# A graph network's attention layers: accumulators kept per head, and a mask's penalty in PSUM

## The reference, cut to what matters

```python
def _gat_layer(x, src, dst, W, a_src, a_dst, b):
    h = (x @ W).reshape(N, H, C)                  # H = 4, C = 24
    alpha_s = jnp.einsum('nhc,hc->nh', h, a_src)
    alpha_d = jnp.einsum('nhc,hc->nh', h, a_dst)
    e = jax.nn.leaky_relu(alpha_s[src] + alpha_d[dst], NEG_SLOPE)
    m = jax.ops.segment_max(e, dst, num_segments=N)
    ex = jnp.exp(e - m[dst])
    den = jax.ops.segment_sum(ex, dst, num_segments=N)
    msg = h[src] * (ex / (den[dst] + 1e-16))[:, :, None]
    return jax.ops.segment_sum(msg, dst, num_segments=N).reshape(N, H * C) + b

x = _layernorm(x + message_layer(x))
y = x
for l in range(3):
    y = jax.nn.relu(_gat_layer(y, src, dst, W[l], att_src[l], att_dst[l], bias[l]))
x = _layernorm(x + y)
```

## Time and profile before

| | us |
|---|---|
| median of 3 runs | 8607.32 (8591.76 to 8612.24) |
| profiled execution | 8603.82 |
| its span | 8601.9 |

### The profile page before, as it was taken

The page is one execution under the profiler, slowest core; times in us unless marked ns, Lnnn a source line. Parts: engine busy times, 40 slices in busy tenths (PEclk is TensorE's granted clock), DMA queues, the critical chain, the costliest instruction groups (busy, mean ns, idle before and its releaser), DMA issues. The chain is left out here.

```text
span 8601.9 us, 131191 instructions
## 1 busy us (share of the span) xinstructions
PE 5700.5 (66%) x27740; PEld 5045.6 (59%) x27740; DVE 4467.6 (52%) x11640; ACT 3999.8 (46%) x8993; POOL 6236.4 (72%) x6545
## 2 busy tenths in 40 slices
PE   6999997777566666666656666666665666666663
PEld 2488886666555555555545555555554555555553
DVE  8977765555544444444444444444454444444446
ACT  5755554444344444444434444444443444444443
POOL 3677777777577777777667777777757777777775
PEclk7555555555566666666666666666666666666666
DMA  5222222222122222222222222222222222222221
GB/s 161 65 49 49 49 48 46 47 46 46 36 42 42 42 42 42 42 42 42 37 44 42 42 42 42 42 42 42 42 38 42 42 42 42 42 42 42 42 42 32
DMA packets 290250, 394.16 MB, mean 46 GB/s; under 512 B 176392, under 2 KB 183960, under 8 KB 287984
## 3 DMA queue, kind: packets, MB, share of 16 engines
q0 software_dynamic: 206976, 330.75, 20.1%
q1 hardware_dynamic: 61176, 46.25, 2.2%
q10 hardware_dynamic: 22024, 16.47, 0.8%
HBM read 367.38 MB, written 25.63 MB: 46 GB/s over the span
## 5 line engine op out<-in xcount | busy, mean ns | idle before, releaser
L637 POOL DMA_INDIRECT store<-table_a,idx x4851 | 4615.1, 951 | 1556.5 <-issue 1463.3
L1286 PE MATMUL ps<-store,work 128*128 x9744 | 1769.7, 352 | 945.1 <-ACT work L1218 942.5
L1286 PEld LDWEIGHTS ps<-store,work 128*128 128x128 f32 x9744 | 1646.2, 262 | 1132.3 <-issue 1128.1
L1269 PE MATMUL ps<-ident,work 128*128 128x128 f32 x4872 | 1148.9, 409 | 1371.7 <-ACT work L1225 1371.1
L779 POOL DMA_INDIRECT store<-table_m,idx x1617 | 1532.8, 948 | 615.1 <-issue 478.8
L1225 ACT ACTIVATE work<-work,small 128x896 f32<-128x896 f32 x696 | 725.1, 1042 | 2415.4 <-DVE store L1143 2379.3
L1269 PEld LDWEIGHTS ps<-ident,work 128*128 128x128 f32 x4872 | 920.4, 215 | 1453.8 <-issue 1359.3
L1151 DVE CUSTOM_DVE_ANT_0 work<-work,ps 128x896 f32<-128x896 f32 x696 | 756.6, 1087 | 1231.3 <-issue 937.8
L1162 DVE SCALAR_TENSOR_TENSOR work<-dstf,store,select 128x224 f32 x696 | 314.0, 451 | 1891.4 <-SPq L600 1887.5
L1277 PE MATMUL ps<-ident,work 128*128 128x128 f32 x4872 | 1090.3, 395 | 111.8 <-DVE work L1172 111.8
L1277 PEld LDWEIGHTS ps<-ident,work 128*128 128x128 f32 x4872 | 980.6, 217 | 115.4 <-DVE work L1172 115.4
(11 more groups left out here) (251 smaller groups left out, 5029.8 us busy)
## 6 DMA issues: line engine op xcount, KB each, us to landing
store<-table_a,idx POOLq DMA_INDIRECT x4851
store<-table_m,idx POOLq DMA_INDIRECT x1617, 2.5
work<-edge_parts ACTq DMA_DIRECT2D x232, 45.5 KB
edge_parts<-store SPq DMA_DIRECT2D x6, 1617.0 KB, 11.5
work<-edge_parts SPq DMA_DIRECT2D x50, 192.0 KB
table_a<-work SPq DMA_DIRECT2D x12, 606.0 KB, 6.3
work<-table_b ACTq DMA_DIRECT2D x232, 12.0 KB
idx<-in_src_dram SPq DMA_DIRECT2D x116, 28.0 KB, 1.8
```

Source lines behind the costliest of these rows:

```text
L637: pool.indirect_dma_start(rows[:, k % RING, j, 0:width], None, table, bass.IndirectOffsetOnAxis(ap=idx[:, k // CHUNK, at:at + 1], axis=0)) ...
L1269: last = pe.transpose(ps[:, 4 + j // 4, (j % 4) * P:(j % 4 + 1) * P], prob[:, par, j, :], ident[:])
L1286: last = pe.matmul(ps[:, 6 + par, 0:D + 1], probT[:, par, j, :], rows_of(at("slot", 3))[:, j, 0:D + 1], start=(j == 0), stop=(j == TPG - 1))
```

## The change

*Rows of 28 words.* In the accumulators each partition keeps only its own head's 24 channels and its sum, then the three other words: ROW_A = 28. For this each head's channels have a one of their own behind them in the table: DX = 4 x 25 = 100 columns and 4 logits, TW = 104 for 101, WX = 108 for 105 with the destination logits. The weights are laid out to match; those of layers 2 and 3 (`w_heads`) take an input of 128 partitions (32 a head, 24 of use and a one in the last head's 25th, ONE_AT), so they are loaded head by head, eight loads on ScalarE's queue, and the bias by four on SP's.

*Parts.* ScalarE copies the four diagonal blocks (32x25 each) unscaled from PSUM, and two select values to `held`; VectorE multiplies both in one instruction of 128x50 (`of_rows`), and accumulates rows of 25 words. Both parities now lie in PSUM bank 6.

*Penalty.* `pen` lies in PSUM bank 7 instead of SBUF.

*Between the passes and at the end.* `fold` is gone. `normalise` works on all 128 partitions: divisors and product for a piece of the windows into `heads` (32 words a window), and one transpose of 32x32 blocks on VectorE, which leaves XH, (head, channel) in partitions and nodes in columns. ScalarE adds the bias with Relu in place, TensorE multiplies. TensorE doesn't turn tiles here any more; it does at the end, where XH is turned back, and VectorE adds the residual from PSUM. GpSimd has no part in either. The table is written in nine pieces instead of five between the passes.

*Message to first pass.* The sum over the nodes is shared between VectorE (3600 columns) and ScalarE; ScalarE keeps every second product; GpSimd clears 198 x 4 and 196 x 8 words a partition instead of 19800; the first two index loads of a pass are issued by SP in the block before it (`first_indices`), ahead of the table's writes.

```diff
-TW = D + 1 + H
+CW = C + 1
+DX = H * CW
+TW = DX + H
-ROW_A = D + 4
+ROW_A = C + 4
...
+                    for l in range(1, LAYERS):
+                        for h in range(H):
+                            load(act, w_heads[h * WA:h * WA + C, l - 1, 0:DX].rearrange("i (g c) -> i g c", c=CW)[:, :, 0:C],
+                                 Wl[l, h * C:(h + 1) * C, :].rearrange("i (g c) -> i g c", c=C), s_heads)
...
+        def first_indices(sp, of):
+            for b in range(2):
+                sp.dma_start(idx[:, b, :], src[:, b * IW:(b + 1) * IW]).then_inc(of[f"idx{b}"], 16)
...
-                    for c in range(2):
-                        load_indices(c, c)
...
-        pen = work[:, 8 * GE + 224:8 * GE + 224 + TPG * WA].rearrange("p (j n) -> p j n", j=TPG)
+        pen = ps[:, 7, 0:TPG * WA].rearrange("p (j n) -> p j n", j=TPG)
...
                     dve.wait_ge(s["parted"], k + 1)
+                    dve.tensor_tensor(of_rows, part_sums[:, par].unsqueeze(1).broadcast_to([P, 2, CW]),
+                                      held[:, par].unsqueeze(2).broadcast_to([P, 2, CW]), ALU.mult).then_inc(s["rows_ready"], 1)
+                    dve.wait_ge(s["rows_ready"], k + 1)
                     for v in range(2):
-                        a = big[:, bass.ds(at("row", 4) + v * ROW_A, D + 1)]
-                        last = dve.scalar_tensor_tensor(a, a, keep[:, par, v:v + 1], part_sums[:, par, v, :], ALU.mult, ALU.add)
+                        a = big[:, bass.ds(at("row", 4) + v * ROW_A, CW)]
+                        last = dve.scalar_tensor_tensor(a, a, keep[:, par, v:v + 1], of_rows[:, v, :], ALU.mult, ALU.add)
...
                     act.wait_ge(s["o_ready"], k + 1)
-                    for v in range(2):
-                        last = nc.scalar.activation(part_sums[:, par, v, :], ps[:, 6 + par, 0:D + 1], ACT.Copy,
-                                                    scale=selects[:, bass.ds(at("table", 3) + WA + v, 1)])
-                    last.then_inc(s["parted"], 1)
+                    for h in range(H):
+                        of_head = slice(h * WA, (h + 1) * WA)
+                        nc.scalar.activation(part_sums[of_head, par, :], ps[of_head, 6, P * par + h * CW:P * par + (h + 1) * CW], ACT.Copy)
+                    nc.scalar.activation(held[:, par], selects[:, bass.ds(at("table", 3) + WA, 2)], ACT.Copy).then_inc(s["parted"], 1)
...
+        def normalise(dve, link, b0, b1):
+
+            w0, w1 = QUARTERS * tiles[b0][0], QUARTERS * (tiles[b1 - 1][-1] + 1)
+            r = rden[:, w0:w1]
+            link(dve.tensor_scalar(r, acc[:, w0:w1, C], 1e-16, None, ALU.add))
+            link(dve.reciprocal(r, r))
+            link(dve.scalar_tensor_tensor(r, acc[:, w0:w1, NEGMAX], FLOOR, r, ALU.is_lt, ALU.mult))
+            link(dve.tensor_tensor(heads[:, w0:w1, 0:C], acc[:, w0:w1, 0:C], r.unsqueeze(2).broadcast_to([P, w1 - w0, C]), ALU.mult))
+            return dve.transpose(XH[:, w0 * WA:w1 * WA], heads[:, w0:w1, :].rearrange("p w c -> p (w c)"))
+
+        PIECES = [(0, 1), (1, 4), (4, 7), (7, 10), (10, NB)]
...
+                nc.scalar.activation(other_half, acc_m[0:D, HALF:N], ACT.Copy, accum_out=small[0:D, 41:42]).then_inc(s_half, 1)
...
-                link(dve.tensor_reduce(total, acc_m[0:D, 0:N], AX.X, ALU.add))
+                link(dve.tensor_reduce(total, acc_m[0:D, 0:HALF], AX.X, ALU.add))
+                dve.wait_ge(s_half, 1)
+                link(dve.tensor_tensor(total, total, small[0:D, 41:42], ALU.add))
...
-                pool.memset(big, 0.0).then_inc(s_zero, 1)
+                pool.memset(acc[:, :, C:], 0.0).then_inc(s_zero, 1)
+                pool.memset(heads[:, :, C:], 0.0)
...
+        ENDS = [(0, 1), (1, 4), (4, 7), (7, 10), (10, 12), (12, NB)]
...
+                for p in range(NE + 2):
+                    if p < NE:
+                        relu(p)
+                    if 1 <= p < NE + 1:
+                        root(p - 1)
+                    if p >= 2:
+                        norm(p - 2)
...
+                for p in range(NE + 2):
+                    if p < NE:
+                        normalise(dve, link, *ENDS[p]).then_inc(s_last, 1)
+                    if p >= 2:
+                        scale(p - 2)
+                    if 1 <= p < NE + 1:
+                        measure(p - 1)
```

282 lines of the change are left out of this document (147 added, 135 removed).

## The result

The changed kernel takes 8509.96 us (median of 4 runs, 8505.25 to 8517.46) where the kernel before took 8609.78 beside it: a ratio of 0.9889, with an interval of 0.9877 to 0.9902, or 96 us less by the ratio (the two medians lie 100 us apart). The forecast was 8502 in a range of 8470 to 8540. The profiled execution took 8511.5 us with a span of 8509.7; the one of before 8603.8 and 8601.9. So the two profiles to be compared differ by 92 us, where the sum was 105.

A forecast was written before the change was run, and what follows sets the result against it. GpSimd issuing gathers back to back was taken as the bound, 8.09 of 8.60 ms. Gathers -34, drain behind the passes +3, start +0.5, ahead of passes -12.7, between -38, last stage -24: -105 us, so 8502 us, range 8470 to 8540.

The forecast's parts named there:

- The gathers: In the passes: slow gathers come from the penalty's write to SBUF; moving it to PSUM wins 34 us.
- rival 1: In the passes: slow gathers come from L1172 or a table read, so the 34 us stay; 8536 us, chance 0.09.
- The idle time: Between gathers: the later mask turn fits the pacing's 2.1 us margin, so GpSimd waits no longer; cost 0.
- Rival 3: In the passes: a mask turn 2.5 us later makes the pacing the bound, +275 us to 8777; chance 0.03.
- Ahead of the passes: Message stage to first pass: shared sum, shorter memset and earlier index loads together win 12.7 us (6 to 15).
- the memset: Ahead of the first pass: L1449 waits for GpSimd's memset of 19800 words; clearing fewer wins 8.7 us.
- The shared sum: Ahead of the first pass: splitting the sum over 6250 columns between VectorE and ScalarE wins 2.6 us.
- The 1.9 us for the index loads: Ahead of the first pass: issuing index loads before the table's writes removes idle time before the gather, -1.9 us.
- Between the passes: Two stretches between passes: shorter folds, TensorE late next, and earlier table writes and indices; -38 us, drain counted apart.
- the last stage: After the last accumulate: 59 us instead of 83, as VectorE's folds shrink; -24 us (-12 to -33), drain counted apart.
- ScalarE's queue: In the last stage: Relu queued behind normalisations makes VectorE's adds wait, +5 us.
- The start: Kernel start: extra loads share DMA engines with the edge data, memsets cost nothing; +0.5 us (0 to +4).

The follow-up runs named there:

- e1: Kernel before with only the mask's penalty moved to PSUM; ratio 0.9969 to the kernel before, 27 us less.
- e2: Changed kernel with the penalty written to SBUF again; ratio 1.0062 to the kernel before.
- e8: Changed kernel with accumulate ahead of the mismatch and the penalty in SBUF again; ratio 1.0158 to the kernel before.
- e3: Changed kernel with gathers paced one step looser, waiting for the mask turned one step earlier; ratio 0.9873 to the kernel before.
- e4: Changed kernel with VectorE's accumulate moved ahead of the mismatch; ratio 0.9855 to the kernel before.
- e12: Changed kernel with only the new multiply ahead of the mismatch, the two adds behind it; ratio 0.9874 to the kernel before.
- e6: Changed kernel with GpSimd's memset over all 19800 words again; ratio 0.9895 to the kernel before.
- e7: Changed kernel with the first two index loads of a pass behind the barrier again; ratio 0.9883 to the kernel before.
- e9: Changed kernel unaltered, in another launch; ratio 0.9900 to the kernel before.

## Why the prediction was right, and where it was not

**The gathers (-34; -31.6).** The mechanism was right, and e1 shows it by itself: 37 us. That it came out in the changed kernel too was in part luck, for the price of rival 1 was wrong. I wrote of L1172 "it runs 1.09 us, over two gathers, and only the one at L1169 is long", and priced the case in which the penalty stays costly at 34 us. The row was right, the reading wrong: L1172 did no harm because it ended within 0.13 us of a gather's start, and the change itself moves it. By e2 the penalty's place is worth 134 us in the changed kernel, and without it the rest of the change would have been slower than the kernel before. What the prediction called untested, that the penalty's output in PSUM is enough, e1 shows: the instruction is 0.39 instead of 0.27 us long, and the gathers beside it are unharmed. I had moved the mask by "0.2 to 0.5 later" and asked only whom the delay keeps waiting, not what it would now stand beside.

A rule bore on this. The Trainium skill, "SBUF — State Buffer", section "Who interferes with whom", says that a VectorE instruction with two SBUF inputs contends with a GpSimd instruction that reads SBUF; a gather reads its column of indices there. The runs agree (0.90 us longer in e8, nothing with one input in PSUM). The same section infers that such an addition doesn't hold up the writing of descriptors. The gathers here are held up by it all the same; whether at their reading or at their writing, no run shows.

**The idle time (0; +19).** This is the step that failed: "2.1 us of margin ... the added 0.05 to 0.5 us fit. Cost 0". The way was named correctly (accumulate, then L1225, then the turns), the delay too (0.2 us), the margin not: 1.74 us of it are needed in every tenth group, so 0.4 were left of the 2.1. And it was read from one step, of group 75, which is none of these; their smallest margin before was 1.69, so in the tightest of them nothing was left. Rival 3 was thus the true mechanism at a fifteenth of its price: 18 us, not 275. It had a delay of 2.5 us, and it charged all 687 groups where only 66 can pay. Shown by e3, e4 and e12, and by the table of margins.

**Ahead of the passes (-12.7; -14.6 and -13.7).** Right in mechanism for the memset, by e6. The shared sum wins only because the memset is gone. The 1.9 us for the index loads are not shown (e7). The stretch itself took 65.2 us in e2 and 78.3 in the changed kernel with the same code, so that its total comes out within 2 us of the forecast is in part luck.

**Between the passes (-36; -45 and -43) and the last stage (-23; -31).** VectorE's share was right (18 us; 17.4), the transposes cost 1.78 us for 1536 elements, 1.16 ns each against 1.07 assumed. Missed: TensorE, put at the low clock with 24.5 us (its own terms, 3 + 21, make 24), had 22 of its 98 instructions at a granted clock of 0.5 and the other 76 at 1.0 in the first block, so VectorE was late next (21.4). The prediction had the high clock as its larger bound, -18 for this part against a measured -16. In the last stage ScalarE's queue did not hold VectorE up by the 5 us reckoned: VectorE ran from 8459.17 to 8499.19, 40.0 us, with no wait to speak of before its end.

**The start (+0.5; +7.3 and -1.0).** In e9 the loads and memsets cost nothing that shows. The 8 us between the two launches come from TensorE's pace; the kernel before was never seen at the slow one, but in two profiles only.

In sum the median came out 8 us above the forecast because an unforeseen 19 us in the gaps and 7 in the start were mostly paid by 17 us more won in the folds. That is luck: errors of 26 and 17 us against each other, in a sum of 105. And the rivals missed one case: without the penalty in PSUM the rest of the change loses (e2).

## What to carry to other kernels

When an edit moves an instruction on an engine that shares something with the bound engine, sort the bound engine's durations by the distance between the two starts, and read where the edit will put it: a collision that is free today may be only 0.2 us away. A margin in front of a pacing wait is to be read over all groups and beside the gaps, sorted by the group's place too: here margins of 0.8 us cost nothing in nine groups of ten, and in the tenth anything under 1.74 did. The smallest margin seen without a gap would have been no safe bound. Work that waits for nothing new belongs in front of the wait for landed data, not behind it: that order alone was worth 25 us here.

## What the runs showed of the hardware

- A VectorE instruction with all operands in SBUF makes a GpSimd gather that begins while it runs longer, by the time that it runs on past the gather's start, less 0.13 us (1381 of 1390 meetings): begun 0.06 us ahead, L1202 costs the gather 0.90 us; 0.03 us ahead it costs it nothing, and VectorE 0.05 us (e8). The penalty, with one input, does the same (before), and doesn't with its output in PSUM (e1).
- VectorE's 96x96 scaling stood still for 11.2 us behind a GpSimd memset of 19800 words (e6), and ended with it.
- A group's semaphore that comes under 1.74 us before its first gather shows as idle time before the second one, but in every tenth group of a pass only (all 36 gaps of 0.05 us or more in the changed kernel, all 33 in e9, all 18 in e12).
- The same kernel ran its last 98 TensorE instructions of the node products in 11.18 us in one launch (e9) and in 21.22 in another (the first profile), 0.11 against 0.22 us each, with the same TensorE rows up to 69 us (to 0.3 us). That is the pace of the two clock levels in the stretch between the passes (0.11 and 0.21). The view's granted clock is 1.00 for both from 69 to 95 us, so the pace is the evidence. Between the message stage and the first pass the like happened: busy time by stretch (columns as above), e2 and then the changed kernel:

```profile
2185.00:2205.00 20.00, 19.01 (x143) 18.26 (x143) 18.67 (x108) 17.57 (x49) 4.15 (x8) 0.83 0.11 33
```
```profile
2185.00:2205.00 20.00, 19.25 (x93) 18.85 (x92) 14.21 (x78) 13.13 (x36) 3.30 (x7) 0.50 0.05 14
```

The code of this stretch is the same; e2's took 65.2 us and the changed kernel's 78.3. Differences of this size between two single profiles, in a stretch bound by TensorE, say nothing of an edit.
